# Retention plus ternary FFN on one core: key-value states gathered right behind the scores, summed by one running sum

## What is computed

```python
def _retention(q, k, v):            # per batch and head, C = CHUNK = 64, N = 8 blocks
    def step(S, x):
        qc, kc, vc = x
        attn = jnp.einsum('bhid,bhjd->bhij', qc, kc) * D            # D: decay, causal
        o_intra = jnp.einsum('bhij,bhje->bhie', attn, vc)
        o_inter = jnp.einsum('bhid,bhde->bhie', qc * decay_q[None, :, :, None], S)
        S_new = decay_s[None, :, None, None] * S + jnp.einsum('bhjd,bhje->bhde', kc * decay_k[None, :, :, None], vc)
        return (S_new, o_intra + o_inter)
...
xn = _layernorm(x, axis=-1)
# attention: q, k, v = xn @ Wq, xn @ Wk, xn @ Wv;  _retention(q, k, v) @ Wo
# ffn: h = bitlinear(xn, w_fc) + gate * (xn @ v.T @ fast_b.T @ u.T);  r = max(h, 0);  bitlinear(r * r, w_proj)
x = x + _L0_attn_ref(xn, ...) + _L0_ffn_ref(xn, ...)
```

## Time and profile before

| what | value |
|---|---|
| median of 3 runs | 128.42 us (127.86 to 129.88) |
| the profiled execution | 129.01 us, of which 127.04 us are the span of the trace |
| PE, matrix products | 117.0 us busy, 92% of the span |
| DVE | 99.2 us, 78% |
| ACT | 78.7 us, 62% |
| POOL | 64.0 us, 50% |
| granted TensorE clock | 0.997 over the span |

### The profile page before, as it was taken

One profiled execution on the slowest core, in us unless ns is written; L12 is line 12 of the kernel. 1 busy time (PEld: TensorE's weight loads), 2 busy tenths in 40 slices (PEclk: granted clock), 3 DMA queues, 4 the chain that ended last, 5 costly groups with the idle time before them and its releaser, 6 DMA issues.

```text
span 127.0 us, 6564 instructions
## 1 busy us (share of the span) xinstructions
PE 117.0 (92%) x2860; PEld 92.8 (73%) x2860; DVE 99.2 (78%) x261; ACT 78.7 (62%) x158; POOL 64.0 (50%) x60
## 2 busy tenths in 40 slices
PE   4979999988999999499999999999999999499991
PEld 4425869856688778377788778878897889377890
DVE  0788795489799969858699979896999799729832
ACT  3265669967871897227972897188738774382910
POOL 7099803984439161923439252916193529544400
PEclk9999999999999999999999999999999999999998
DMA  3849920000023000400023001300020002000202
GB/s 105 296 149 320 389 92 34 0 3 5 8 90 81 5 0 23 145 7 0 0 92 74 0 0 53 112 0 0 0 83 0 0 0 83 0 5 0 88 5 83
DMA packets 3357, 7.71 MB, mean 61 GB/s; under 512 B 384, under 2 KB 896, under 8 KB 3216
## 3 DMA queue, kind: packets, MB, share of 16 engines
q1 hardware_dynamic: 2880, 7.01, 16.3%
q10 hardware_dynamic: 464, 0.50, 1.2%
HBM read 5.42 MB, written 2.10 MB: 59 GB/s over the span
## 4 chain that ended last, share of the span: by engine, by line
PE 80%; DVE 10%; issue 4%; ACT 2%; POOL 1%; DVEq 0%; POOLq 0%
PE ps_work L659 10%; PE ps_score L735 8%; PE ps_work L663 7%; PE ps_work L660 7%; PE ps_score L705 6%; PE ps_score L747 5%; PE ps_score L781 5%; PE ps_y L761 4%; PE ps_y L762 4%; PE ps_score L720 3%; DVE sums_of L532 3%; PE ps_turn L668 3%; PE ps_y L765 2%; DVE xn L491 2%; PE ps_turn L692 1%
## 5 line engine op out<-in xcount | busy, mean ns | idle before, releaser
L300 POOL TENSOR_TENSOR sq_lo<-square,sq_hi 128x512 fp32r<-128x512 f32 x31 | 39.8, 1295 | 36.2 <-ACT sq_hi L356 36.2
L347 ACT ACTIVATE square<-ps_work 128x512 f32<-128x512 f32 x32 | 19.1, 596 | 23.1 <-PE ps_work L663 22.6
L516 DVE TENSOR_TENSOR scores<-ps_score,cst 128x512 f32<-128x512 f32 x32 | 20.3, 682 | 1.6 <-PE ps_score L705 1.6
L305 POOL TENSOR_TENSOR q_pair<-q_dec,cst 128x1024 f32<-128x1024 f32 x7 | 13.3, 1894 | 15.9 <-DVE q_dec L501 15.9
L356 ACT ACTIVATE sq_hi<-square 128x512 fp32r<-128x512 f32 x32 | 20.1, 627 | 0.1
L352 ACT ACTIVATE square<-square 128x512 f32<-128x512 f32 x32 | 18.9, 630 | 0.1
L491 DVE TENSOR_SCALAR xn<-x_in,mean_var,rstd 128x128 f32<-128x128 f32 x32 | 14.9, 528 | 0.3
L659 PE MATMUL ps_work<-xn_hi,w_hi 128*128 128x512 f32 x32 | 14.3, 447 | 0.4 <-issue 0.4
L735 PE MATMUL ps_score<-scores,v_pad 64*32 64x64 f32 x1024 | 12.5, 225 | 1.6 <-issue 1.6
L663 PE MATMUL ps_work<-xn_lo,w_hi 128*128 128x512 f32 x32 | 12.6, 394 | 0.0
L660 PE MATMUL ps_work<-xn_hi,w_lo 128*128 128x512 f32 x32 | 12.6, 393 | 0.0
(11 more groups left out here) (123 smaller groups left out, 238.6 us busy)
## 6 DMA issues: line engine op xcount, KB each, us to landing
x_in<-x_tok SPq DMA_DIRECT2D x8, 256.0 KB, 3.4
resid<-x_feat SPq DMA_DIRECT2D x1, 2048.0 KB, 7.7
out_feat<-resid SPq DMA_DIRECT2D x7, 256.0 KB
po_in<-ffn_weights SPq DMA_DIRECT2D x1, 320.0 KB, 3.2
fc_in<-ffn_weights SPq DMA_DIRECT2D x1, 256.0 KB, 3.7
q_table<-q_decay SPq DMA_DIRECT2D x1, 256.0 KB, 3.5
wqvk<-qvk_weights ACTq DMA_DIRECT2D x1, 192.0 KB, 3.9
cst<-const ACTq DMA_DIRECT2D x1, 129.0 KB, 3.9
```

Of the source, the lines that this page charges most:

```text
L300: nc.gpsimd.tensor_tensor(sq_lo[p][:, f, :], square[p][:, f, :], sq_hi[p][:, f, :].bitcast(F32), ALU.subtract).then_inc(lo_ready, 1)
L347: nc.scalar.activation(square[b.parity][:, f, :], ps_work[f % 2][:], ACT.Relu).then_inc(relu_ready, 1)
L516: nc.vector.tensor_tensor(scores[:, g].rearrange("p t s i -> p (t s) i"), ps_score[:, g].rearrange("p (a i) -> p a i", i=BLK), causal.unsq ...
```

## The change

The states of a batch are gathered right behind its scores, in the same pass of the loop, between the hidden tiles. They go to the banks `ps_turn` and `ps_y` (now the two halves of `ps_both`), so they no longer wait for masks, but `turn_xn` of the next batch, which overwrites `ps_turn`, now waits until DVE has taken them (`states_taken`). DVE writes the masked states back to PSUM, block by block within each feature, and one `tensor_tensor_scan` (`sum_states`) makes all running sums: it multiplies the sum so far by `restart` (1, and 0 where a new feature starts) and adds the next state. `own_values` and `carry` of a batch now stand in front of the projections of the next one, so `carry` comes in the same pass, and the split of the attention's output (`high_o`, `low_o`) with it. POOL spreads `q_dec` behind all four low squares and no longer between them. DVE and ACT work out the statistics two batches ahead (`later`): `statistics` in front of `decay_q`, `variance` behind it. The helper `zero_products` becomes `place_program`, with 12 small products at the start, 27 behind the first transpose, 14 in front of the first `carry` and 15 in front of the last `own_values`.

```diff
+def over_middle(engine, body):
+    with engine.Fori(0, NB // 2 - 2) as half:
+        body(Batch(half, 1), True)
+        body(Batch(half, 2), True)
+    body(Batch(NB // 2 - 2, 1), True)
+    body(Batch(NB // 2 - 2, 2), False)
...
-        sums_of = [sb(f"sums_of{k}", [P, PAD + NBLK, GW]) for k in (1, 2, 4, 8)]
+        state_sums = sb("state_sums", [P, GW * NBLK])
+        restart = sb("restart", [P, GW * NBLK])
...
-        ps_turn = pb("ps_turn", [P, SEQ])
-        ps_y = pb("ps_y", [P, SEQ])
+        ps_both = pb("ps_both", [P, ROWS, SEQ])
+        ps_turn, ps_y = ps_both[:, 0, :], ps_both[:, 1, :]
+        w1_bank = ps_score[:, NG - 1, :]
+        masked_states = ps_score[:, ROWS, 0:GW * NBLK]
...
@@ POOL
             def body(b):
-                for f in range(2):
+                for f in range(NF):
                     low_square(b, f)
                 spread_q(b.step(1))
-                for f in range(2, NF):
-                    low_square(b, f)
...
@@ ACT
-            def body(b):
+            def body(b, more):
                 take_relu(b, 0)
                 take_relu(b, 1)
-                root(b.step(1))
                 take_square(b, 0)
+                high_square(b, 0)
                 take_square(b, 1)
-                high_square(b, 0)
-                high_o(b.step(-1))
                 take_relu(b, 2)
+                take_relu(b, 3)
+                round_xn(b.step(1))
                 high_square(b, 1)
-                round_xn(b.step(1))
-                take_relu(b, 3)
                 take_square(b, 2)
+                high_square(b, 2)
                 take_square(b, 3)
-                high_square(b, 2)
+                high_square(b, 3)
+                high_o(b)
                 copy_k(b.step(1))
                 copy_k_tok(b.step(1), 0)
-                high_square(b, 3)
                 copy_k_tok(b.step(1), 1)
+                if more:
+                    root(b.step(2))
...
@@ DVE
             def take_states(b):
 
+                dve.wait_ge(scores_ready, b.count(NG, 1))
                 dve.wait_ge(state_done, b.count(1, 1))
                 nc.vector.tensor_tensor(
-                    sums_of[0][:, PAD:].rearrange("p (t r) e -> p t r e", r=ROWS),
-                    ps_score[:, ROWS:2 * ROWS, 0:NT * GW].rearrange("p r (t e) -> p t r e", e=GW),
-                    pair_mask.unsqueeze(1).unsqueeze(1).broadcast_to([P, NT, ROWS, GW]),
-                    ALU.mult).then_inc(state_step, 1)
-
-            def add_states(b, k):
-                dve.wait_ge(state_step, b.count(3, k + 1))
-                nc.vector.tensor_tensor(
-                    sums_of[k + 1][:, PAD:-1], sums_of[k][:, PAD:-1], sums_of[k][:, PAD - 2 ** k:-1 - 2 ** k],
-                    ALU.add).then_inc(state_step if k < 2 else state_ready, 1)
+                    masked_states.rearrange("p (e t r) -> p r t e", t=NT, r=ROWS),
+                    ps_both[:, :, 0:NT * GW].rearrange("p r (t e) -> p r t e", e=GW),
+                    pair_mask.unsqueeze(1).unsqueeze(1).broadcast_to([P, ROWS, NT, GW]),
+                    ALU.mult).then_inc(states_taken, 1)
+
+            def sum_states(b):
+                dve.wait_ge(states_taken, b.count(1, 1))
+                nc.vector.tensor_tensor_scan(state_sums[:], restart[:], masked_states, 0.0, ALU.mult,
+                                             ALU.add).then_inc(state_ready, 1)
...
-            def body(b):
-                before, after = b.step(-1), b.step(1)
-                statistics(after)
-                statistics_done(after)
-                take_states(before)
-                variance(after)
-                for k in range(3):
-                    add_states(before, k)
+            def body(b, more):
+                before, after, later = b.step(-1), b.step(1), b.step(2)
                 for step in range(4):
                     inverse_root(after, step)
                 normalise(after)
-                low_o(before)
+                mask_scores(b, ROWS)
+                mask_scores(b, 0)
+                take_states(b)
+                for g in (1, 3):
+                    mask_scores(b, g)
                 low_xn(after)
-                for g in MASK_ORDER[:2]:
-                    mask_scores(b, g)
+                sum_states(b)
                 finish(before, ps_y)
+                if more:
+                    statistics(later)
+                    statistics_done(later)
                 decay_q(after)
-                for g in MASK_ORDER[2:]:
-                    mask_scores(b, g)
-                for side in range(2):
-                    take_v(after, side)
+                if more:
+                    variance(later)
+                low_o(b)
+                take_v(after, 0)
+                take_v(after, 1)
...
@@ PE
-            def turn_xn(b):
+            def turn_xn(b, before=None):
                 pe.wait_ge(xn_ready, b.count(1, 1))
+                if before is not None:
+
+                    pe.wait_ge(states_taken, before.count(1, 1))
...
-                        ins = mm(ps_score[rows, r, t * BLK:(t + 1) * BLK], sums_of[3][rows, PAD + blk - 1, :],
+                        ins = mm(ps_score[rows, r, t * BLK:(t + 1) * BLK], state_sums[rows, blk - 1:GW * NBLK:NBLK],
...
+            own_values(first)
+            place_program(14, ps_score[:, NG - 1, :], ident)
+            carry(first)
+
+            def hidden_and_scores(b):
 
                 pe.wait_ge(q_ready, b.count(1, 1))
                 hidden(b, 0)
                 pe.wait_ge(k_ready, b.count(1, 1))
                 hidden(b, 1)
+                pe.wait_ge(o_lo_ready, b.count(1, 0))
+                score(b)
+                gather_states(b)
                 hidden(b, 2)
                 hidden(b, 3)
+
+            def body(b):
+                before, after = b.step(-1), b.step(1)
+                hidden_and_scores(b)
+                turn_xn(after, b)
+                second_product(before, ps_y, range(NF))
+
+                pe.wait_ge(relu_ready, b.count(NF, NF))
                 output_product(before, ps_y)
-                project_q(after, b)
-                project_k(after, b)
+                own_values(b)
+                carry(b)
+                project_q(after)
+                project_k(after)
                 project_vk(after, 0)
                 project_vk(after, 1)
-                gather_states(b)
-                own_values(b)
...
+            hidden_and_scores(last)
+            pe.wait_ge(states_taken, last.count(1, 1))
+            second_product(before, ps_y, range(NF))
             output_product(before, ps_y)
+            pe.wait_ge(scores_ready, last.count(NG, NG))
+            pe.wait_ge(state_ready, last.count(1, 1))
+            place_program(15, ps_score[:, NG - 1, :], ident)
             own_values(last)
             carry(last)
+            pe.wait_ge(relu_ready, last.count(NF, 3))
+            for f in range(NF):
+                last_second(f)
```

174 lines of the change are left out of this document (77 added, 97 removed).

## The result

The changed kernel takes 139.38 us (median of 4 runs, 138.57 to 140.48) against 128.79 us for the kernel before on the same chip: ratio 1.085, 95% interval 1.074 to 1.097. It is slower, by twice what was forecast. The profiled execution took 138.57 us with a span of 136.5 us, where the sum of the prediction gave 132.0. Some executions of a kernel take over 1.5% longer than its fastest; the ratios leave these out, the medians (of e5 and e9 above all) don't.

A forecast was written before the change was run, and what follows sets the result against it. PE bound the loop before (13.10 us a batch); afterwards a chain over DVE, POOL and PE would: 26.8 + 6 x 14.8 + 15.5 = 131.1, plus 0.9 program waits, span 132.0. Time 128.42 + 5.0 = 133.4 us, range 126.5 to 136.0.

The forecast's parts named there:

- the waits for program: PE standing still for its instructions: 0, 1.64 us as before, or twice; taken as 0.9 us in the sum.
- PE's work: PE in the loop: one change of product size less per batch, giving 12.9 us a batch if nobody waits.
- Steps 1 to 3: From `q_dec`'s start T: spreading at T + 0.83 holds `var_eps`, so `low_o` starts at T + 2.67, `normalise` at T + 4.83.
- The rival that `var_eps` isn't held: In the loop on DVE: `var_eps` passes the spreading, PE bounds at 12.9 us a batch; span 120.4, time 121.8; chance 0.20.
- Step 4: In the loop: POOL's low square starts at about T + 5.2; `normalise` loses 0.9 us and ends near T + 6.75.
- The rival that it escapes: In the loop: `normalise` escapes the low square, a batch takes 13.9 us, the time is 128.0; chance 0.23.
- Steps 5 and 6: Masks and `take_states` let the transpose start at T + 8.4; PE takes 6.4 to the next `q_dec`: 14.8 us a batch.
- The running sum: On DVE behind `low_xn`: 0.6 us, allowing 0.3 to 1.3, costing nothing; dropping the three additions pays little.
- Start and end: Loop starts at 26.8 us, give or take 0.8; the last batch to the trace's end takes 15.5 against 19.16.
- the case of several places: PE's program waits come in two or three places, or `take_states` is slow: 136 us or more; chance 0.05.
- From the span to the time: Span 132.0 against 127.04 before, so 5.0 us added to the median of 128.42: 133.4 us.

The follow-up runs named there:

- e5: e1 with own values ahead of the projections in the preparation, and fillers moved from there and the last batch to the program's start; 135.12 us, ratio 1.025.
- e9: e1 plus batch 0's own values ahead of the projections, POOL, ACT and DVE reordered at the pipeline's start, 33 fillers in the last batch; 129.23 us, ratio 0.995.
- e1: The changed kernel with the variance moved ahead of the decay of the next queries on DVE in the loop; 130.74 us, ratio 1.020.
- e11: e9 with, in the last batch, no fillers and the own values between two halves of the second product; 125.82 us, ratio 0.974.
- e12: e11 with `finish` and the variance back where the change has them, the variance behind the decay of the next queries; 136.47 us, ratio 1.053.
- e2: The changed kernel with high square 0 put behind square 1 on ACT in the loop; 134.55 us, ratio 1.048.
- e4: The kernel before with only the three additions of the states replaced by one running sum, from SBUF to SBUF; 128.47 us, ratio 1.000.
- e3: The changed kernel with 20 more fillers behind the first transposes and none in the last batch; 138.12 us, ratio 1.075.
- e6: e5 with the variance where the change put it; 142.4 us, ratio 1.105.

## Why the prediction was wrong

The direction and the mechanism in the loop were right; the time was 6.0 us short and outside the range. The step that failed is the last term of the sum, the waits for program; the granted clock, which has no term in it, failed with it.

*PE's work.* Forecast 12.9 us a batch. With the waits gone it is 13.10 to 13.12 (e1, e11): `carry` with weights in steps takes 1.02, not the 0.91 that I took.

*Steps 1 to 3.* Right to 0.1 us: spreading at T + 0.83, `low_o` at T + 2.67, `normalise` at T + 4.72 (4.83 forecast). e1 takes `var_eps` away from the spreading, and with it the whole wait goes; e12 puts it back. The rival that `var_eps` isn't held is refuted. (Its sum of 120.4 also starts from 26.6, where the main sum has 26.8.)

*Step 4.* Low square at T + 5.28 (5.2 forecast), the masks behind `normalise` at T + 6.83 (6.75). e2 shows that the low square is the cause. The rival that it escapes came true in part: in the changed kernel it met the low square in four of the loop's six batches (period 15.2, and 15.8 with a program wait in it) and escaped in two (14.13 in one, against 13.9 forecast; the other has the program wait of 1.72 in it). Why it escapes in batches 1 and 3, in e12 too, I did not pursue.

*Steps 5 and 6.* The transposes came at T + 8.6 (8.4), and PE took 6.6 from there (6.4): 0.1 for `carry` and 0.1 for one more change from wide to small products in front of `own_values`. The period where they met is 15.2, not 14.8. The loop took 90.6 us, and 6 x 14.8 was 88.8. Less the program waits in it that is 90.6 - 1.72 - 0.34 = 88.5; e12, whose loop has none, took 89.6. So with two batches that escaped, two errors about cancel, which is luck.

*The running sum.* 0.68 us, nobody waits for it, `take_states` 0.42: as forecast. e4 bears out that it doesn't pay.

*Start and end.* Without program waits 28.66 - 1.16 = 27.5 (26.8 forecast, inside its 0.8) and 17.23 - 0.94 = 16.3 (15.5). The fillers were mis-sized: 15 of them last 0.58 from start to start of what follows, not 0.25, being two products each.

*The waits for program: the term that failed.* "I take 0.9", from one wait in the earlier trace rows, with the case of several places at 0.05. They are 1.16 + 1.72 + 0.34 + 0.94 = 4.2, so by subtraction 3.3 of the 4.5 us between the sum and the span; the other 1.2 are start and end (0.7 + 0.8) less 0.3 in the loop. e3 shows that these waits follow the count of instructions. e12, the changed kernel with them gone, the start put in order and 29 fillers less (which last some 1.0 us), has a span of 132.6 us, 3.9 shorter, and the sum of the prediction without its 0.9 was 131.1. So the waits cost nearer to 2.9 than 4.2: in batch 1 DVE's chain holds PE up in e12 too (0.72 us, period 14.5, against 15.2 with 1.72 of program wait in it). Either way the term is three to five times too small, and the largest single error.

The error of reasoning was to treat the term as luck ("I cannot say to where"). The wait of the earlier trace rows stands before instruction 1985, which fixes the edges, and the dense runs of the new order can be laid against them: `own_values` with `carry`, 368 instructions in 2.4 us, and scores with states, 240 in 1.8, with only two hidden tiles between one and the next at the start. That would have shown the waits of 1.16 and 0.94, whose blocks were used up in 2.0 and 1.7 us. The other two, like that of the earlier trace rows, stand behind blocks of 3.7 to 4.6 us whose successor was fetched late; no count shows these.

*From the span to the time.* The other 1.5 of the 6.0 us lie outside the span: I added 1.4 us to it, and the profiled execution had 2.1; and the median is 0.8 above that execution. Its granted clock was 1.00, while the other three executions had 0.988 and spans of 137.2 to 138.5 us. A clock of 0.988 over 137 us is an estimated 1.6 us of lost work. The prediction put this at nothing and gave no reason.

## What to carry to other kernels

Here a four-element instruction from SBUF to SBUF on DVE, queued behind the release of a spreading of 1.90 us on POOL, lasted until that one's end (1.74 us for 0.17). Look at what stands right behind each semaphore that starts POOL, and put it ahead (8.6 us here for one exchange of places). Where a program isn't yet loaded, count instructions: 15 blocks of 256 that small products used up in 1.7 to 2.0 us ended with PE standing still for 0.4 to 1.8 us, ahead of the loop, in its first pass and behind it. In the last batch wide products in between cured it (e11) where fillers didn't (e9). And price both separately, since mending the one can expose the other (e5, e6).

## Unexpected in the hardware

- Waits for program came to 0.3 to 2.3 us each, 27 of them in 12 of the 14 traces, every one at an edge. The first instruction of the next block ran 2.2 to 2.8 us after the start of that block's packet on the instruction queue. The packet had started anywhere from 0.3 us ahead of the crossing into the block before to 4.8 us behind it. So a block needn't be dense to end in a wait: 12 of the 27 had lasted 3.7 to 5.9 us, with the packet 1.9 us late or more. And six blocks as short as 1.6 to 1.9 us had no wait, their packet having started 0.3 to 0.8 us ahead. What delays a packet isn't known.
- After two such waits (e1, e3), or one of 2.26 us (e6), the granted clock fell to its lower level (0.50) for 3 to 4 us, though PE worked all of that time. In the changed kernel's profiled execution, with 1.16 and 1.72 us of waits, and in e2, with 1.30 and 1.46, it stayed at 1.00, and in e4 it fell at 12.3 us with no such wait. That the waits bring it on is a guess.
- A spreading holds a DVE instruction between SBUF tiles exactly as a low square does (1.74 against 0.17 in the preparation); `low_o`, the masks and the running sum, which read PSUM, were not lengthened by POOL in any trace (a mask lasted 0.67 to 0.69 with POOL beside it or not; the sum from SBUF in e4 was lengthened once: 1.24 against 0.68).
- Writing the masked states in steps takes 0.42 into PSUM (the changed kernel) and 0.67 into SBUF (e4).
